# When TensorE and ScalarE read their run-time values: moving register loads and one wait in a sorted mixture-of-experts kernel

## The chip, the cores and the metric

The kernel runs on one core of a Trainium2 chip. The metric is the device time of one execution in microseconds (us). The engines are named as the profile names them: PE is TensorE's matmul side and PEld its weight loads, DVE is VectorE, ACT is ScalarE, POOL is GpSimd, SP is SyncE. A "q" behind an engine (PEldq, ACTq) marks an instruction of that engine's sequencer, which hands instructions to the engine and does the register work itself.

## The reference, cut to what matters

A state-space layer, two layer norms and a mixture of experts over 4096 rows of 256 numbers:

```python
def _L0_attn_ref(x, A, B, C, D, gamma, beta):
    state = jnp.tanh(state @ A.T + xb_t)          # scan over the sequence, xb = x @ B.T
    y = states @ C.T + D * x + x
    return layernorm(y) * gamma + beta
def _L0_ffn_ref(x, ...):
    scores = sigmoid(x @ router_weight.T)         # 8 experts in 2 groups of 4
    # the better group of 4 is chosen, of it the best two experts; comb = their weights
    g, u = x @ w_gate[e], x @ w_up[e]
    routed = sum_e comb[:, e] * ((silu(g) * u) @ w_down[e])
    shared = (silu(x @ sw_gate) * (x @ sw_up)) @ sw_down
    return routed + shared
x = layernorm(x + _L0_attn_ref(x, ...))
x = layernorm(x + _L0_ffn_ref(x, ...))
```

## The kernel before

The 4096 rows are 32 tiles of 128, in 8 batches g of four tiles. After the scan (up to about 75 us of the span) each batch is projected, normalised (`rows`, `scale_rows`, `sum_rows`, `sum_moments`, `normalise`), transposed (`turn_x2`), scored (`logits`, `scores`), routed (`choose_group`, `choose_two`, `weigh`), and **sorted by group**: rows that choose group 0 are copied to the front of `x2_sorted`, the others to its back. A permutation matrix made by `sort_tiles` is multiplied in (`permute`), and ScalarE copies each tile twice, to two places that only the data decide: `offsets` reads those places from `zeros_i` into registers with `value_load`, and `put` copies with `main.placed` as its count. The routing weights go the same way: `turn_comb` multiplies them, `put_comb` copies them into `comb_sorted`, with the count `main.comb_placed`.

The experts' work runs over the sorted rows in ten **passes** i of 2, 2, 4, 4, 4, 4, 4, 4, 2 and 2 tiles. Passes 0 to 8 use one group each and have five **units** j (the shared expert at j = 0, then four routed ones); pass 9 has nine. Which columns and which group a pass takes is decided by the data: GpSimd's `plan(i)` writes them to `pass_i` (count `pass_known`), and TensorE's `take(i)` reads them into registers with two `value_load`s. A unit is `up` (12 matmuls of gate and up projection), ScalarE's silu (L747), VectorE's products (`inner`, L1122 for the shared expert, L1125 and L1129 for routed ones, the latter counting `h_done`), ScalarE's copy to 16 bit (`high`, L756), GpSimd's rest (`low`, L1338) and `down`. The 54 units n = 5i + j are software pipelined: at step n TensorE does `up_main(n + 1)`, `front_early(n)`, `down_main(n - 1)`, `front_late(n)`.

The routing of batch g is spread over the pass before it by `due(n, ahead)`, in an order that each engine's program writes out by hand. In a pass: `scores`, `choose_group` at j = 0; `sort_tiles`, `offsets`, first two `permute`s at j = 1 (the latter on TensorE); the first two `put`s, the other two `permute`s and `choose_two` at j = 2; the other two `put`s, `weigh`, `turn_comb` and `plan` at j = 3, and ScalarE's `normalise` of the batch after; `put_comb`, `turn_x2` and its copies at j = 4. In `turn_x2` the transposes for k = 0 wait for `comb_placed`, as they reuse the bank of the weights (except after the last batch, when there is no `turn_x2`). At the head of a pass `ids` needs the sorted weights, and so do the `spread`s of the units behind it; the products of `up` for j = 0 need only the sorted rows. GpSimd's own long operations at this place are `rows_in` (L1283 and L1288, ahead of passes 2, 3 and 4 only), `low` (L1338) and `low_rows` (L1333). VectorE's `score` (L1023) and `choice` (L1024) are the first steps of `choose_group`.

Of the kernel before, what the change touches and what calls it, by code (L numbers as in the profile page):

```python
# [20 lines left out]
def ssm_moe_kernel(nc, x, A, B, C, D, gamma, beta, router_weight, correction_bias,  # L21
# [8 lines left out]
    T4 = 4  # L30
# [11 lines left out]
    with ExitStack() as ctx:  # L42
# [168 lines left out]
        main, again = Sems("", 3), Sems("again_", 1)  # L211
# [28 lines left out]
        EP = 1 + EPG  # L240
        TILES = [T4 // 2] * 2 + [T4] * (G - 2) + [T4 // 2] * 2
        EXPERTS = [EP] * (G + 1) + [E1]
        KNOWN = list(range(G)) + [G - 1] * 2
        NPASS = len(TILES)
        NP = NPASS - 1
# [3 lines left out]
        UNITS = [(i, j) for i in range(NPASS) for j in range(EXPERTS[i])]  # L249
# [16 lines left out]
        def due(n, ahead, first=0):  # L266

            g, odd = divmod(n + ahead, EP)
            return g if odd == 0 and first <= g < G else None
# [51 lines left out]
        def _(pe):  # L321
# [91 lines left out]
            def permute_main(g, t):  # L413
                if t == 0:
                    pe.wait_ge(perm_ready, g + 1)
                    pe.wait_ge(main.x2_low, g + 1)
                    if g:
                        pe.wait_ge(main.y1_done, 2 * min(g + 2, G))
                if t >= 2 and g:

                    pe.wait_ge(main.placed, g * 2 * T4 + 2 * (t - 1))
                permute(t, perm[:, t, :], ps_rows(g, t), main)
# [14 lines left out]
            def up(n, m, e, group, col, w, sems):  # L437

                if not isinstance(n, int) or n >= 1:
                    pe.wait_ge(sems.silu_done, n)  # L440
                for which, (ps, done) in enumerate(((ps_g, sems.up_g), (ps_u[m % 2], sems.up_u))):
                    if which and (not isinstance(n, int) or n >= 2):
                        pe.wait_ge(sems.gu_done, before(n, m, 1))
                    first = True
                    for k in range(KT):
                        for px, pw in PART:
                            start = e * KT * I + k * I
                            part = bass.ds(group * (EPG * KT * I) + start, I) if group is not None else slice(start, start + I)
                            last = pe.matmul(ps[:, 0:w], up_rows[which][pw][:, part],  # L449
                                             x2_sorted[:, k * 2 + px, bass.ds(col, w)],  # L450
                                             start=first, stop=(k == KT - 1 and (px, pw) == PART[-1]))
                            first = False
                    last.then_inc(done, 1)
# [78 lines left out]
            def take(i):  # L532

                pe.wait_ge(pass_known, i + 1)
                col = pe.value_load(pass_i[0:1, i, 0:1], min_val=0, max_val=N - TILES[i] * P)
                group = pe.value_load(pass_i[0:1, i, 1:2], min_val=0, max_val=1) if i < NP else None
                pe.wait_ge(main.comb_placed, (KNOWN[i] + 1) * 2 * T4)
                return col, group

            taken_at = {}  # L540

            def up_main(n):
                i, j = UNITS[n]
                if j == 0:
                    taken_at[i] = take(i)
                col, group = taken_at[i]
                w = TILES[i] * P
                up(n, n, j, group if j else None, col, w, main)
                if j == 1:
                    pe.wait_ge(main.ids_ready, i + 1)  # L550
                if j:
                    spread(routed(i, j), j, group, col, w, main)
                else:
                    pe.wait_ge(main.h_done, routed(i, 1))
                    ids(col, TILES[i], main)
# [10 lines left out]
            def front_early(n):  # L566

                g = due(n, EP + 1, 2)
                if g is not None:
                    logits(g, main)  # L570
                g = due(n, EP, 1)
                if g is not None:
                    places(g)
                g = due(n, EP - 1, 1)
                if g is not None:
                    for t in (0, 1):
                        permute_main(g, t)
                g = due(n, EP - 2, 1)
                if g is not None:
                    for t in (2, 3):  # L580
                        permute_main(g, t)
                g = due(n, EP - 3, 1)
                if g is not None:
                    turn_comb(g)
# [12 lines left out]

            pe.wait_ge(weights_ready, 3)
            pe.wait_ge(back_made, 1)
            up_main(0)  # L600
            for n in range(NALL):
                if n + 1 < NALL:
# [13 lines left out]
            with pe.If(all_met == 0):  # L616
# [20 lines left out]
                with pe.Fori(0, G // 2) as two:  # L637
                    for half in range(2):
                        g = two * 2 + half
# [18 lines left out]
                        for e in range(E1):  # L658
                            n, m = g * E1 + e, half * E1 + e
# [15 lines left out]
        def _(act):  # L675
# [36 lines left out]
                nc.scalar.activation(th[:, :, :], ps_misc[0][:, 0:T4 * E].rearrange("p (t e) -> p t e", t=T4),  # L712
                                     ACT.Tanh, scale=0.5 / XS).then_inc(sems.th_done, 1)

            def offsets(g):
                act.wait_ge(offsets_known, g + 1)
                return [act.value_load(zeros_i[0:1, g * T4 + t:g * T4 + t + 1], min_val=0, max_val=(g * T4 + t) * P)  # L717
                        for t in range(T4)]

            def behind_copies(done, copy):  # L720

# [76 lines left out]
            normalise(1, 1, main)  # L798
            scores(0, main)
            keep_turned(1, main)  # L800
            at = offsets(0)
            for t in range(T4):
                put(0, t, at)
            scores(1, main)
# [2 lines left out]
            for n, (i, j) in enumerate(UNITS):  # L807
                w = TILES[i] * P
                silu(n, n, w, main)
                if n:  # L810
                    before_i, before_j = UNITS[n - 1]
                    high(n - 1, n - 1, routed(before_i, before_j) if before_j else None, TILES[before_i] * P, main)
                g = due(n, EP, 1)
                if g is not None:
                    high_rows(g, g % 3, main)
                    if g > 1:
                        scores(g, main)
                if j == 0 and i >= 2:
                    finish(i - 2, i % 2, TILES[i - 2], main)
                if j == 1 and i:  # L820
                    sums((i - 1) % 2, TILES[i - 1], (i - 3) % 3, sent_by(i - 3), unit(i, 0), main)
                g = due(n, EP - 1, 1)
                if g is not None:
                    at = offsets(g)
                g = due(n, EP - 2, 1)
                if g is not None:
                    put(g, 0, at)
                    put(g, 1, at)
                g = due(n, EP - 3, 1)
                if g is not None:  # L830
                    put(g, 2, at)
                    put(g, 3, at)
                g = due(n, EP + 2, 2)
                if g is not None:
                    normalise(g, g % 3, main)
                g = due(n, 1, 1)
                if g is not None:
                    put_comb(g, at)
                g = due(n, EP + 1, 2)
                if g is not None:  # L840
                    keep_turned(g, main)
                if (i, j) == (NP, EP):
                    finish(NP - 1, (NP - 1) % 2, TILES[NP - 1], main)
            i, j = UNITS[-1]
# [393 lines left out]
        def _(pool):  # L1238
# [157 lines left out]
            for n, (i, j) in enumerate(UNITS):  # L1396
                if n:
                    low(n - 1, n - 1, TILES[UNITS[n - 1][0]] * P, main)
                g = due(n, EP, 1)
                if g is not None:  # L1400
                    low_rows(g, g % 3, main)
                    note_tiles(g, main)
                g = due(n, 2 * EP - 1, 3)
                if g is not None:
                    deviations1(g, g % 3, main)
                g = due(n, 2 * EP - 2, 3)
                if g is not None:
                    deviations2(g, g % 3, main)
                g = due(n, EP - 3, 1)
                if g is not None:  # L1410
                    plan(g)
                g = due(n, 1, 1)
                if g is not None:
                    watch(g)
                if j == 4 and i:
                    deviations3(i - 1, (i - 1) % 2, TB[i - 1], TILES[i - 1], main)
                if 1 <= i <= G - 5 and j == 4:
                    rows_in(i + 4)
                if j in (0, 1) and i >= 2:
                    half = TILES[i - 2] // 2  # L1420
                    send(i - 2, i % 2, (i - 2) % 3, TB[i - 2], TILES[i - 2], main, range(j * half, (j + 1) * half))
                if (i, j) == (NP, EP):
                    send(NP - 1, (NP - 1) % 2, (NP - 1) % 3, TB[NP - 1], TILES[NP - 1], main)
                if (i, j) == (G - 1, 1):
                    plan(G)
                    plan_last()
# [54 lines left out]
```

## Time and profile before

| | |
|---|---|
| median of 3 runs | 355.1 us (353.13 to 357.61) |
| the profiled execution | 353.79 us, span 352.0 us, so 1.8 us lie outside the span |
| PE busy | 302.4 us, 86% of the span |
| DVE, ACT, POOL busy | 221.0, 185.6, 207.3 us |
| mean granted clock of TensorE | 0.942 of full |
| passes 0 to 9 | from 88.96 us to the end |

No engine is busy all the time; over the passes the work goes round between them, so the question at each place is which wait ends last. Times in the rows are us from the start of the span.

### The profile page before, as it was taken

To read this page: it belongs to the slowest core of one execution; us is meant where nothing else is said; L and a number is where in the kernel's file an instruction comes from. 1 tells how busy PE (TensorE), PEld (TensorE's weight loads), DVE (VectorE), ACT (ScalarE), POOL (GpSimd) and SP (SyncE) were. 2 spreads that over 40 slices of the span, in tenths; PEclk is the share of its full clock that TensorE was granted. 3 is DMA by queue.
4 is the path that set the end of the run, shared out by engine and by line. 5 is a ranking of instruction groups with operands and counts; after the bars stand their busy time and mean duration, and the time that the engine had idled before them with its cause. 6 is when DMAs were issued, how large, how long until landed. Compare 5 with 4: busy or idle time off the path is not lost.

```text
span 352.0 us, 7374 instructions
## 1 busy us (share of the span) xinstructions
PE 302.4 (86%) x2255; PEld 227.5 (65%) x2255; DVE 221.0 (63%) x671; ACT 185.6 (53%) x442; POOL 207.3 (59%) x326
## 2 busy tenths in 40 slices
PE   5999999946696777998998899899899799998940
PEld 4998888846475664764765656476566556787830
DVE  2235998965563893797599499679835723453520
ACT  2565322645357176358349637756864853545420
POOL 8898012453323448648937984678864655578632
PEclk9999999985689986999999999999999999999995
DMA  6992000000000000000000000000001000011001
GB/s 188 343 339 99 0 3 0 2 0 0 0 4 0 2 2 0 19 15 2 0 33 2 2 30 32 2 32 32 0 17 47 3 32 30 7 57 60 32 4 34
DMA packets 6810, 13.19 MB, mean 37 GB/s; under 512 B 1000, under 2 KB 3568, under 8 KB 6768
## 3 DMA queue, kind: packets, MB, share of 16 engines
q1 hardware_dynamic: 5232, 8.47, 7.5%
q0 software_dynamic: 1536, 4.20, 3.4%
q8 instruction: 22, 0.36, 0.4%
q14 instruction: 20, 0.16, 0.2%
HBM read 8.47 MB, written 4.19 MB: 36 GB/s over the span
## 4 chain that ended last, share of the span: by engine, by line
PE 46%; DVE 23%; issue 8%; ACT 7%; POOL 5%; SPq 5%; DMA 2%; ACTq 2%; POOLq 0%; DVEq 0%
PE bank L449 18%; PE bank L472 8%; PE bank L356 5%; PE bank L362 4%; DVE st L964 3%; SPq L290 3%; PE bank L392 3%; PE bank L374 2%; DVE wg L1125 2%; DMA xres<-in_L_attn_x_dram 2%; DVE wu L1129 2%; PE bank L385 2%; POOL out_dram L1382 2%; ACT comb_sorted L740 2%; ACTq L717 2%
## 5 line engine op out<-in xcount | busy, mean ns | idle before, releaser
L1338 POOL TENSOR_TENSOR h<-wu,h 128x512 f16<-128x512 f32 (+1 forms) x54 | 51.0, 947 | 64.0 <-ACT h L756 63.7
L449 PE MATMUL bank<-xT,wg 128*128 x324 | 66.9, 346 | 10.9 <-issue 5.0
L747 ACT ACTIVATE wg<-bank,g_un 128x512 f32<-128x512 f32 (+1 forms) x54 | 32.1, 594 | 79.5 <-PE bank L449 51.9
L472 PE MATMUL bank<-wd,h 128*128 (+1 forms) x504 | 64.7, 275 | 2.1 <-POOL h L1338 2.1
L449 PE MATMUL bank<-xT,wu 128*128 x324 | 65.4, 340 | 0.0
L472 PEld LDWEIGHTS bank<-wd,h 128*128 128x128 f16 x504 | 47.5, 99 | 9.8 <-POOL h L1338 2.6
L449 PEld LDWEIGHTS bank<-xT,wg 128*128 (+1 forms) x324 | 31.3, 101 | 31.8 <-issue 14.7
L1125 DVE SCALAR_TENSOR_TENSOR wg<-bank,u_un,wg 128x512 f32<-128x512 f32 (+1 forms) x44 | 27.3, 620 | 36.1 <-PE bank L449 15.6
L449 PEld LDWEIGHTS bank<-xT,wu 128*128 (+1 forms) x324 | 32.8, 101 | 24.4 <-issue 1.3
L356 PE MATMUL bank<-xT,BT 128*128 128x128 f32 x256 | 39.8, 278 | 0.0
L731 ACT ACTIVATE xT<-bank 128x512 f32 (+1 forms) x64 | 33.6, 613 | 7.9 <-PE bank L409 7.1
L356 PEld LDWEIGHTS bank<-xT,BT 128*128 128x128 f32 x256 | 34.2, 194 | 0.1
L756 ACT ACTIVATE h<-wu 128x512 f16<-128x512 f32 (+1 forms) x54 | 28.7, 532 | 0.9 <-DVE wu L1129 0.9
L1129 DVE TENSOR_TENSOR wu<-bank,wg 128x512 f32<-128x512 f32 (+1 forms) x44 | 25.1, 570 | 1.5
L1136 DVE CAST row_id<-bank 128x4 int32<-128x4 f32 (+1 forms) x10 | 1.6, 161 | 38.4 <-PE bank L464 38.4
L1333 POOL TENSOR_TENSOR wd<-xskip,wd 128x1024 f16<-128x1024 f32 x8 | 17.0, 2130 | 13.1 <-ACT wd L696 13.1
L964 DVE BATCH_NORM_STATS2 st<-xskip 128x6 f32<-128x256 f32 x64 | 22.4, 413 | 0.4
L1382 POOL DMA_INDIRECT out_dram<-z_odd,row_id x16 | 18.4, 1149 | 5.7 <-issue 3.2
L1283 POOL TENSOR_TENSOR xskip<-xres,D_bc 128x1024 f32<-128x1024 f32 x8 | 18.8, 2353 | 1.6 <-PE bank L345 1.6
L1382 POOL DMA_INDIRECT out_dram<-wd,row_id x16 | 16.7, 1046 | 5.1 <-issue 3.2
L683 ACT ACTIVATE states<-bank 128x128 f32<-128x128 f32 x32 | 8.9, 278 | 20.4 <-PE bank L362 20.1
L1288 POOL TENSOR_TENSOR xres<-xres,beta_bc 128x1024 f32<-128x1024 f32 x8 | 18.8, 2356 | 1.1
(186 smaller groups left out, 553.8 us busy)
## 6 DMA issues: line engine op xcount, KB each, us to landing
xres<-in_L_attn_x_dram SPq DMA_DIRECT2D x7, 512.0 KB, 6.1
wd<-in_L_ffn_w_down_dram SPq DMA_DIRECT2D x1, 1024.0 KB, 7.1
xres<-in_L_attn_x_dram SPq DMA_DIRECT2D x2, 256.0 KB, 3.0
out_dram<-wd,row_id POOLq DMA_INDIRECT x16, 2.5
out_dram<-z_odd,row_id POOLq DMA_INDIRECT x16, 2.5
states<-in_L_attn_B_dram SPq DMA_DIRECT2D x1, 128.0 KB, 2.5
D_bc<-in_L_attn_D_dram SPq DMA_DIRECT2D x1, 128.0 KB, 5.0
beta_bc<-in_L_attn_beta_dram SPq DMA_DIRECT2D x1, 128.0 KB, 6.4
```

The costliest lines, as they stand in the source:

```text
L356: pe.matmul(ps_scan[s % 2][:, 0:P], BT[:, k, :], xT[:, k, tile, :], start=(k == 0), stop=False)
L449: last = pe.matmul(ps[:, 0:w], up_rows[which][pw][:, part], x2_sorted[:, k * 2 + px, bass.ds(col, w)], start=first, stop=(k == KT - 1 and ...
L472: last = pe.matmul(ps_y[t // 2][:, (t % 2) * DM:(t % 2 + 1) * DM], h16[:, m % 3, ph, t * P:(t + 1) * P], down_rows[pw][:, rows], start=(fi ...
L731: nc.scalar.activation(x2_sorted[:, :, bass.ds(where, P)], ps_rows(g, t)[:, :].rearrange("p (a c) -> p a c", a=2 * KT), ACT.Copy).then_inc ...
L747: nc.scalar.activation(sg[:, m % 2, 0:w], ps_g[:, 0:w], ACT.Silu, scale=g_un[:, 0:1]).then_inc(sems.silu_done, 1)
L756: nc.scalar.activation(h16[:, m % 3, 0, 0:w], h[:, m % 2, 0:w], ACT.Copy).then_inc(sems.h_high, 1)
L964: nc.vector.bn_stats(st[:, st_k, t, :], src(t)).then_inc(st_sem, 1)
L1125: nc.vector.scalar_tensor_tensor(gu[:, m % 2, 0:w], ps_u[m % 2][:, 0:w], u_un[:, 1:2], sg[:, m % 2, 0:w], ALU.mult, ALU.mult).then_inc(sem ...
L1129: nc.vector.tensor_tensor(h[:, m % 2, 0:w], ps_comb[:, 0:w], gu[:, m % 2, 0:w], ALU.mult).then_inc(sems.h_done, 1)
L1283: nc.gpsimd.tensor_tensor(xskip[:, n * T4:(n + 1) * T4, :], xres[:, n * T4:(n + 1) * T4, :], D_bc[:, :].unsqueeze(1).to_broadcast([P, T4, ...
L1338: nc.gpsimd.tensor_tensor(h16[:, m % 3, 1, 0:w], h[:, m % 2, 0:w], h16[:, m % 3, 0, 0:w], ALU.subtract).then_inc(sems.h_low, 1)
L1382: nc.gpsimd.indirect_dma_start(out_rows, bass.IndirectOffsetOnAxis(row_id[:, ring, t:t + 1], 0), z2s[par][:, t, :], None, bounds_check=N - ...
```

## The change

Four moves, no arithmetic changed. (1) `take(i + 1)`, TensorE's two register loads for the next pass, is issued at j = 3 of pass i ahead of `turn_comb` and `down`, not at the head of the next pass; `take(0)` stands before the first `up`. (2) The wait for `comb_placed` moves from `take` behind the `up` of the pass' unit 0; that `up` waits for `placed` in its place. (3) ScalarE's `offsets`, four register loads at j = 1, become two at j = 2 and two at j = 3, each pair right ahead of the two `put`s that use it. (4) GpSimd's `plan(g)` moves one unit up, from j = 3 to j = 2, and ahead of `deviations2`.

```diff
@@ take(i)
                 group = pe.value_load(pass_i[0:1, i, 1:2], min_val=0, max_val=1) if i < NP else None
-                pe.wait_ge(main.comb_placed, (KNOWN[i] + 1) * 2 * T4)
                 return col, group
@@ up_main(n)
                 if j == 0:
-                    taken_at[i] = take(i)
+                    pe.wait_ge(main.placed, (KNOWN[i] + 1) * 2 * T4)
                 col, group = taken_at[i]
                 w = TILES[i] * P
                 up(n, n, j, group if j else None, col, w, main)
+                if j == 0:
+                    pe.wait_ge(main.comb_placed, (KNOWN[i] + 1) * 2 * T4)
@@ front_early(n)
                     for t in (2, 3):
                         permute_main(g, t)
+                i, j = UNITS[n]
+                if j == EP - 2 and i < NP:
+                    taken_at[i + 1] = take(i + 1)
                 g = due(n, EP - 3, 1)
                 if g is not None:
                     turn_comb(g)
@@ TensorE, before the loop over the units
+            taken_at[0] = take(0)
             up_main(0)
@@ ScalarE
-            def offsets(g):
+            def offsets(g, tiles):
                 act.wait_ge(offsets_known, g + 1)
                 return [act.value_load(zeros_i[0:1, g * T4 + t:g * T4 + t + 1], min_val=0, max_val=(g * T4 + t) * P)
-                        for t in range(T4)]
+                        for t in tiles]
@@ ScalarE, loop over the units
-                g = due(n, EP - 1, 1)
-                if g is not None:
-                    at = offsets(g)
                 g = due(n, EP - 2, 1)
                 if g is not None:
+                    at = offsets(g, (0, 1))
                     put(g, 0, at)
                     put(g, 1, at)
                 g = due(n, EP - 3, 1)
                 if g is not None:
+                    at += offsets(g, (2, 3))
                     put(g, 2, at)
                     put(g, 3, at)
@@ GpSimd, loop over the units
+                g = due(n, EP - 2, 1)
+                if g is not None:
+                    plan(g)
                 g = due(n, 2 * EP - 2, 3)
                 if g is not None:
                     deviations2(g, g % 3, main)
-                g = due(n, EP - 3, 1)
-                if g is not None:
-                    plan(g)
```

## Rows read from the trace of the kernel before

**Rows 1.** The list of waits: who waited for whom, total us, times, longest
```profile
ACT wg L747 <- issue: 27.6, 7, 6.5
PE bank L449 <- issue: 5.0, 6, 1.0
PE bank L430 <- DVE comb L1086: 4.8, 5, 1.5
PE bank L449 <- ACT comb_sorted L740: 4.4, 2, 2.6
```

**Rows 2.** Timeline of PE: first products of passes 0, 1, 2, 3 and 7; brackets: idle before
```profile
88.96 1.46 PE L449 MATMUL bank<-xT,wg 128*128 x6 [2.56 <-ACT comb_sorted L740]
...
111.37 0.83 PE L449 MATMUL bank<-xT,wg 128*128 x6 [0.86 <-issue]
...
137.08 2.74 PE L449 MATMUL bank<-xT,wg 128*128 x6 [0.48 <-issue]
...
166.81 1.47 PE L449 MATMUL bank<-xT,wg 128*128 x6 [1.00 <-issue]
...
281.59 1.47 PE L449 MATMUL bank<-xT,wg 128*128 x6 [1.86 <-ACT comb_sorted L740]
```

**Rows 3.** Register loads of take for pass 4, by line, window 194 to 196.6
```profile
L535 PEldq TENSOR_LOAD <-pass_i x1: 308/308/308, 194.9 to 194.9; - x1
L536 PEldq SEQ_ASSERT  x1: 18/18/18, 196.2 to 196.2; - x1
```

**Rows 4.** Timeline, pass 0: last copies of rows; silu behind the loads
```profile
83.68 3.53 ACT L731 ACTIVATE xT<-bank 128x512 f16<-128x512 f32 x7
...
100.34 0.47 ACT L747 ACTIVATE wg<-bank,g_un 128x256 f32<-128x256 f32 x1 [6.49 <-issue]
```

**Rows 5.** Timeline, pass 4, j = 2 and 3 on PE, DVE and POOL
```profile
214.42 0.75 DVE L1125 SCALAR_TENSOR_TENSOR wg<-bank,u_un,wg 128x512 f32<-128x512 f32 x1
...
214.53 1.47 PE L449 MATMUL bank<-xT,wg 128*128 x6 [0.51 <-ACT wg L747]
...
214.99 1.15 POOL L1338 TENSOR_TENSOR h<-wu,h 128x512 f16<-128x512 f32 x1 [2.54 <-ACT h L756]
...
217.70 0.20 POOL L1313 TENSOR_TENSOR rstd<-mv,eps 128x4 f32<-128x4 f32 x1 [1.56 <-DVE mv L968]
...
220.25 0.69 DVE L1129 TENSOR_TENSOR wu<-bank,wg 128x512 f32<-128x512 f32 x1
...
220.91 0.18 POOL L1362 TENSOR_TENSOR pass_f<-zeros_f,taken 1x1 f32<-1x1 f32 x1
...
222.48 0.29 POOL L1370 TENSOR_SCALAR pass_i<-pass_f 1x1 int32<-1x1 f32 x1
...
222.87 0.40 PE L430 MATMUL bank<-perm,comb 128*128 128x128 f16 x4 [0.81 <-DVE comb L1086]
```

**Rows 6.** Timeline, passes 3 and 4: th, score and choice beside POOL's long operations
```profile
168.59 2.35 POOL L1288 TENSOR_TENSOR xres<-xres,beta_bc 128x1024 f32<-128x1024 f32 x1
170.90 1.16 POOL L1338 TENSOR_TENSOR h<-wu,h 128x512 f16<-128x512 f32 x1
...
171.71 0.38 DVE L1023 TENSOR_SCALAR score<-th 128x32 f32<-128x32 f32 x1 [1.16 <-ACT th L712]
172.02 2.13 POOL L1333 TENSOR_TENSOR wd<-xskip,wd 128x1024 f16<-128x1024 f32 x1
172.13 2.06 DVE L1024 TENSOR_TENSOR choice<-score,cbias_bc 128x32 f32<-128x32 f32 x1
...
198.62 2.36 POOL L1288 TENSOR_TENSOR xres<-xres,beta_bc 128x1024 f32<-128x1024 f32 x1
...
201.43 0.70 DVE L1023 TENSOR_SCALAR score<-th 128x32 f32<-128x32 f32 x1 [1.15 <-ACT th L712]
```

**Rows 7.** Windows over passes 1 and 7 to 8: busy (x count), granted clock
```profile
111.40:137.00 25.60, 20.13 (x159) 16.25 (x159) 19.68 (x71) 14.07 (x35) 12.85 (x28) 0.87 0.01 1
...
281.60:315.30 33.70, 33.69 (x260) 23.79 (x261) 13.84 (x39) 16.38 (x32) 20.52 (x30) 1.00 0.09 33
```
Its columns: length, busy us of PE, PEld, DVE, ACT and POOL, the granted clock of TensorE (1.00 is 2.4 GHz, 0.50 is 1.2 GHz), DMA share and GB/s.

More of the change, by code:

```diff
@@ L800, in _ @@
             keep_turned(1, main)
-            at = offsets(0)
+            at = offsets(0, range(T4))
             for t in range(T4):
```

## The prediction

> **What bounds the kernel now.** I read the list of waits first, then the timeline of PE at the head of each pass, then DVE, ACT and POOL between two heads. The list [rows 1] names what this change is about. PE waits 5.0 us in six places for "issue", which is its own sequencer; 4.4 us in two places for the copied weights; 4.8 us in five places for the weights not yet computed; and ACT waits 27.6 us in seven places for its own sequencer. The timeline [rows 2] shows where: passes 1 to 6 begin with an idle PE of 0.86, 0.48, 1.00, 1.0, 0.85 and 0.85 us behind the last transpose (the three of passes 4 to 6 are not shown, they repeat the row of pass 3 and make up the 5.0), passes 0 and 7 with 2.56 and 1.86 us behind the copies. Those 4.4 us are the only ones at which the wait for `comb_placed` ends last by itself: in passes 2 to 6, and in pass 1, the k = 0 transposes have waited for the same count already, and the change leaves that wait in place.
>
> Between the heads no engine is alone the bound. Over pass 4 the timeline goes PE's products, scores, then VectorE without a gap of note until the weights are done, then PE again. VectorE's L1125 at 214.42 has no bracket, it came straight behind VectorE's own work, while PE's products at 214.53 waited 0.51 us for a silu and `turn_comb` at 222.87 waited 0.81 us for VectorE [rows 5]. So through passes 1 to 4 the loop is head, scores, VectorE's chain, head. In passes 5 to 8 PE has hardly a gap but the heads and is itself the bound; over passes 7 and 8 it is busy for 33.69 of 33.70 us [rows 7].
>
> **Part 1, TensorE's loads (take).** One take runs from 194.9 to 196.2 us, 1.35 us of sequencer time, and the engine stood for 1.0 of it [rows 3], as the sequencer was held until the last wait and could not run ahead. Moved ahead of `turn_comb`, the loads lie behind the `spread` that waits for `h_done`. That product (L1129) ends at 220.94, and `turn_comb` can't start before VectorE's routing weights released it at 222.87 [rows 5]: 1.9 us of cover for 1.35 us of loads, in VectorE's own order, hence the same in every pass that has a `turn_comb`. Cost nothing there; were the cover gone, at most 1.35 us a pass. In passes 7 and 8 there is no `turn_comb`; their two later takes cost between 0 and 1.35 us each, and I take 0, since the lists show no idle PE at the heads of passes 8 and 9 with the loads there today. What the head gives back is the issue wait: 0.86 + 0.48 + 1.00 + 1.0 + 0.85 + 0.85 = 5.0 us, with nothing late behind it, as the `up` of unit 0 needs only sorted rows and registers.
>
> **Part 2, the wait for sorted weights.** Pass 7: its 1.86 us go whole; the copies end before `ids` is due 2.6 us later. Pass 0: `up` now waits for `placed`. Those copies end at 83.68 + 3.53 = 87.21 [rows 4], the products can start at 87.35 instead of 88.96: 1.6 us, not 2.56. Behind the waiting `ids` nothing is held that was not held before. 1.6 + 1.86 = 3.5 us.
>
> **Part 3, ScalarE's loads.** In every pass 0 to 6 the silu of unit 2 stands behind four loads that can't begin before VectorE has written `zeros_i`. With the new order the silu goes ahead. What that is worth is not the 27.6 us: in pass 4 PE gets 0.51 us at 214.53, VectorE nothing, because its L1125 was not waiting [rows 5]. PE's gain then only meets the wait at `turn_comb`, unless VectorE is early too. In pass 0 VectorE itself waits 2.7 us for the silu that starts at 100.34 [rows 4], and ScalarE then runs without a gap to the copied weights. Bounds there are 0.2 us (PE's gap) and 2.7 us (VectorE's); I take 0.7, since the two last `put`s must still follow the `permute`s behind unit 3's products. The first two `put`s begin after two loads instead of after four and two 0.5 us activations, so no `put` becomes later.
>
> **Part 4, plan.** Its seven small operations run from 220.91 to 222.77, 1.9 us [rows 5]. One unit earlier they stand ahead of `deviations2` (L1313), which starts 0.1 us behind its input at 217.70. Today's `low` (L1338) ends at 216.14; plan behind it would end at 218.0 and be 0.4 us late for each of five batches. But that `low` waited 2.54 us for ScalarE's copy, which waited behind the four loads; it now comes about 2.5 us earlier and takes plan with it, to about 215.5. Cost 0; if the cover fails, up to 1.9 us in each of passes 1 to 5. Then `normalise`, the k = 1 transposes, and the silu and the weights' copies queued behind `normalise` on ScalarE are late.
>
> **Part 5, what an earlier head meets on POOL.** In pass 3 `score` (0.38 us) ends 0.03 us after POOL's L1338, and `choice`, issued at 172.13 during L1333 (172.02 to 174.15), takes 2.06 us and ends 0.04 us after it. In pass 4 `score` takes 0.70 and `choice` again 2.06, in a row that repeats pass 3's [rows 6]. Both are small operations that take 0.2 us where nothing of POOL's is running. POOL's L1288, L1338 and L1333 follow each other without a gap, and they start from VectorE's statistics of the pass before, not from PE's head. So a head that comes 1.0 us earlier moves `score` against them. In pass 3: issued at 171.71 - 1.0, that is 0.23 us before L1288 ends at 170.94, done with it; `choice` is then issued during L1338 and done when that ends, at 172.1 instead of 174.19. VectorE wins 2.1 us and is off the path; PE is now next, and what it wins is its 1.0 at the head and the 0.9 us it waited at `turn_comb`. In pass 4 the two gaps are 0.51 and 0.81 us, `score` has only 0.45 us to win to reach L1288's end at 200.98. The Trainium skill (SBUF — State Buffer, "SBUF: two separate sides") says that VectorE and GpSimd share a port pair under an exclusive lock, held for a whole instruction, by which whoever starts first blocks the other. By that rule, the trace agrees that `choice` blocks to L1333's end; it does not say who is next when both wait, and the two readings are my first case and the first rival.
>
> **The sum**, as what each place is early by. Head of pass 1: 1.6 + 0.7 + 0.86 = 3.2. Pass 2's head: 3.2 + 0.48 = 3.7, of which 3.4 pass POOL's row of operations on to VectorE. Head 3: 3.4 + 1.0 = 4.4. Pass 3's `turn_comb`: 4.4 + 0.9 = 5.3. Head 4: 6.3. Pass 4's `turn_comb`: 6.3 + 0.51 + 0.81 = 7.6. Head 5: 7.6 + 0.85 = 8.45. Head 6: 0.85 and a gap of 0.2 at the k = 0 transposes, 9.5. Head 7: 9.5 + 1.86 = 11.3. From there PE runs without a gap [rows 7] and the rest follows it. The profiled execution took 353.79 us, so 353.79 - 11.3 = 342.5; it lies 0.4% below the median of 355.1, and in the median's terms this is **343.8 us**, 3.2% faster.
>
> **Rivals.** (a) *POOL and VectorE make a loop of their own.* If `choice` loses the port to L1333, the 2.1 us aren't won; POOL starts from VectorE and VectorE from POOL's end, and the heads of passes 3 and 4 don't count. Then 3.4 + 0.85 (head 5) + 1.05 (head 6) + 1.86 = 7.1: 346.7, or 348.0 in the median's terms, 2.0% faster. For it: the margin of pass 3 is 0.23 us. Against it: `score`, when waiting at the end of L1338, twice came in ahead of L1333's end. (b) *It is met in one of the two passes*: 9.3 us, 345.8. (c) *TensorE's clock.* The windows show 0.87 granted over pass 1 and 1.00 over passes 7 and 8 [rows 7], and the first six products of pass 2 take 2.74 us against 1.47 in pass 3 [rows 2], the two levels of 1.2 and 2.4 GHz; with the other six it is some 2 us. If the shorter gaps keep the clock at 2.4 GHz there, that and what `choice` wins by it are about 2.5 us more in all: 341. The Trainium skill (TensorE: Matmul & The Clock Gate, Part 1) has the clock follow how busy the array was lately, which would speak for this; the row shows PE busy for only 20.13 of the 25.60 us of pass 1 [rows 7] ahead of the slow products, and the longest wait for VectorE's weights, 1.5 us [rows 1], is among the gaps; VectorE, which makes them, isn't helped. (d) *Slower: plan late.* If POOL reaches `low` no earlier than today, plan pushes `deviations2` by up to 1.9 us in five passes, 9.3 us. With only part 2's and the heads' gain of passes 5 to 7 left that is 353.79 - 7.1 + 9.3 = 356.0, or 357.3, 0.6% slower. It decides from the point where `low` of unit 1 ends less than 1.9 us before the second moments (217.6 in pass 4). The 2.54 us that this `low` waits for ScalarE speak against it. (e) *It does little*: PE's early heads are eaten by other waits (the output's sends on POOL, `low` in the last passes) and 3 to 5 us are left, 350 to 352.
>
> **How the numbers follow.** Chances: forecast 0.40, (a) 0.25, (b) 0.15, (c) 0.08, (d) 0.04, (e) 0.08. Two per cent is about what a measurement of this kernel can tell from no change (its three runs spread by 1.3%). The forecast, (b) and (c) are all beyond 2%, 0.63, and (a) sits on the boundary at 348.0 and gives 0.09 of its 0.25 to faster: 0.72. (a)'s rest, (e) and half of (d) are within, 0.26; slower by over 2% needs (d) with a second cause, 0.02. The range takes in (c) below at 340.5 and (a) with half of its own uncertainty above, 350.
>
> **What would show it.** In the list of waits "PE L449 <- issue" all but gone, and "PE L449 <- ACT comb_sorted" gone; L535's loads just after unit 4's products and before L430, with L430 still released by VectorE. "ACT wg L747 <- issue" gone. `choice` of passes 3 and 4 short, or ended by L1338: forecast; ended by L1333, heads 3 and 4 giving nothing: (a). L1313 starting right behind plan's L1370 and L689 idle for POOL: (d). The first products of pass 2 in 2.6 us: (c). The prediction is wrong if PE waits at L430 grow by what the heads lose, or if the ten heads are early as forecast and the last pass is not.

## The result and the profile after

The changed kernel is faster by one per cent: 350.56 us (median of 4 runs, 349.03 to 351.96) against 355.38 us, ratio 0.9899 with a 95% interval of 0.9855 to 0.9943. In a second set of runs it was 0.9867 [0.9824, 0.9911]. The forecast of 343.8 us and its range of 340.5 to 350.0 both missed it, on the optimistic side; the time lies in the band of rival (e), 350 to 352, which had a chance of 0.08. The profiled execution has a span of 350.1 us against 352.0.

The list of waits of the changed kernel, with the rows that answer to [rows 1]:

```profile
ACT wg L752 <- PE bank L449: 49.0, 32, 3.8
...
PE bank L430 <- DVE comb L1090: 6.9, 6, 1.5
...
PE bank L459 <- DVE wu L1133: 4.7, 8, 1.5
```

The two waits that the change aimed at are gone from TensorE's products: of the 5.0 us of "issue" and the 4.4 us for the copied weights the profile page's group of L449 keeps 1.1 us, for another cause. ScalarE's silu no longer waits for the sequencer; its copies of rows (L736) wait for it for 8.7 us in four places instead. And TensorE's waits for VectorE have grown: `turn_comb` (L430) from 4.8 to 6.9 us, and the `spread` (L459), which waits for VectorE's products of the unit before, from 2.2 to 4.7 us.

```profile
L449 PE MATMUL bank<-xT,wg 128*128 x324 | 65.1, 339 | 1.1 <-ACT xT L736 1.0
```

Where it was lost can be read by laying two points of every pass beside each other in the timelines: the `ids` products (L464), just behind the head of pass p, and `turn_comb` (L430) near its end. Each number is the start in the kernel's profile minus the start in that of before, in us, so -2 is two us early. The last row is the changed kernel's second profile, which began 0.5 us late where the first began 1.2 us late (`turn_comb` of batch 0 at 86.3 and 87.0 instead of 85.8):

| | ids 0 | turn 1 | ids 1 | turn 2 | ids 2 | turn 3 | ids 3 | turn 4 | ids 4 | turn 5 | ids 5 | turn 6 | ids 6 | turn 7 | ids 7 |
|---|---|---|---|---|---|---|---|---|---|---|---|---|---|---|---|
| forecast | -1.6 | | -3.2 | | -3.7 | | -4.4 | -5.3 | -6.3 | -7.6 | -8.5 | | -9.5 | | -11.3 |
| changed | -0.4 | -1.7 | -0.8 | -0.8 | -3.1 | -0.2 | -1.4 | +0.8 | -0.4 | +2.1 | +1.0 | +1.4 | +0.3 | +0.3 | -1.7 |
| again | -1.1 | -2.4 | -3.1 | -2.6 | -4.6 | -2.0 | -3.2 | -1.0 | -2.1 | +0.3 | -0.7 | -0.3 | -1.4 | -1.4 | -3.5 |

The heads from pass 3 on give what they should: from "turn" to the next "ids" the changed kernel wins 1.2 us in passes 3 and 4, 1.0 and 1.1 in passes 5 and 6, and 2.0 in pass 7. The heads of passes 1 and 2 are mixed with TensorE's clock. In the first profile it was granted 0.79 from 104 to 112 us, where the kernel before had 1.00, and head 1 loses 1.0 us; in the second it had 1.00 there too, and head 1 wins 0.6. At the head of pass 2 it is the kernel before that has the low clock (0.58 from 134 to 142 us), so the 2.3 us won there are not the loads' alone. From 145 to 320 us the granted clock is 1.00 in all these profiles. And in every one of passes 2 to 4 the stretch from "ids" to the next "turn", which is VectorE's, takes it away again, with 2.2 to 2.9 us. VectorE is busy for 229.1 us instead of 221.0, with the same 671 instructions. The timeline says which of them became longer. First pass 3, the changed kernel, with VectorE's and GpSimd's rows in order of time (its line numbers are 4 or 5 higher than those of before: L996 is L992, L1342 is L1338):

```profile
170.31 0.47 DVE L1027 TENSOR_SCALAR score<-th 128x32 f32<-128x32 f32 x1 [1.15 <-ACT th L717]
170.70 1.16 POOL L1342 TENSOR_TENSOR h<-wu,h 128x512 f16<-128x512 f32 x1
170.81 1.09 DVE L1028 TENSOR_TENSOR choice<-score,cbias_bc 128x32 f32<-128x32 f32 x1
...
171.82 2.12 POOL L1337 TENSOR_TENSOR wd<-xskip,wd 128x1024 f16<-128x1024 f32 x1
171.94 2.03 DVE L1031 TENSOR_TENSOR more<-choice 128x16 f32<-128x16 f32 x1
...
180.69 1.28 DVE L1118 CAST zeros_i<-zeros_f 1x4 int32<-1x4 f32 x1
180.78 1.17 POOL L1342 TENSOR_TENSOR h<-wu,h 128x512 f16<-128x512 f32 x1
...
181.90 1.65 DVE L996 SCALAR_TENSOR_TENSOR xskip<-xskip,mv,gamma_bc 128x256 f32<-128x256 f32 x4
182.05 3.13 POOL L1366 TENSOR_TENSOR pass_f<-zeros_f,taken 1x1 f32<-1x1 f32 x1
```

Two things are to be seen, beside [rows 6]. `choice` slipped in as forecast: issued at 170.81 during `low`, it ended with it at 171.90, not with `low_rows`. But the next operation, `more`, then stood for 2.03 us until `low_rows` ended at 173.94; before, it took 0.17. Both together end at 173.97, before at 174.40: the slip was worth 0.4 us, not 2.1. And the copy `zeros_i` of four numbers takes 1.28 us, with `low` (L1342) starting 0.09 us behind it and ending 0.02 us ahead of its end. The kernel before has it so:

```profile
181.01 0.15 DVE L1114 CAST zeros_i<-zeros_f 1x4 int32<-1x4 f32 x1
181.08 1.65 DVE L992 SCALAR_TENSOR_TENSOR xskip<-xskip,mv,gamma_bc 128x256 f32<-128x256 f32 x4
...
184.71 1.15 POOL L1338 TENSOR_TENSOR h<-wu,h 128x512 f16<-128x512 f32 x1 [3.63 <-ACT h L756]
```

There `low` came 3.6 us later, since ScalarE's copy that it needs stood behind the four register loads. In pass 2 it is the same (1.31 instead of 0.15); in pass 4 `low` fell on the third of the four L996, which takes 2.02 us (212.58 to 214.60), so that the group takes 3.21 instead of 1.66. This L996 began 0.54 us before the start that is recorded for `low`, and ended 0.30 us behind its end; why it waited although it came first, the rows don't show. In passes 0 and 1 one of VectorE's operations, `zeros_i` and `perm`, pays 0.5 us each in the same way.

```profile
211.79 3.21 DVE L996 SCALAR_TENSOR_TENSOR xskip<-xskip,mv,gamma_bc 128x256 f32<-128x256 f32 x4
...
213.12 1.18 POOL L1342 TENSOR_TENSOR h<-wu,h 128x512 f16<-128x512 f32 x1
```

So the theory behind the experiments, the *port theory*: part 3 takes ScalarE's loads out of the way of `low`, `low` lands on VectorE's operations, and VectorE, whose chain the head waits for, loses 1.2, 1.1 and 1.5 us in passes 2, 3 and 4. Beside it stands the rival (a) of the prediction, the loop of POOL and VectorE, for the heads of passes 2 to 4. The rivals to both: that VectorE's work bounds these passes whatever one does; and that the moved loads, or the copies that now wait for them, hold something up.

### The profile page after: what moved, and what is told of

Its sections match the earlier page's. It is cut to its first block, busy times and chain, and to the rows that moved or that the text cites. A ratio compares the mean times of both kernels' runs of the same rounds, so it can differ in the third digit from the quotient of the medians.

```text
span 350.1 us, 7384 instructions
## 1 busy us (share of the span) xinstructions
PE 301.0 (86%) x2255; PEld 227.7 (65%) x2255; DVE 229.1 (65%) x671; ACT 188.3 (54%) x442; POOL 216.6 (62%) x326
## 4 chain that ended last, share of the span: by engine, by line
PE 42%; DVE 27%; issue 8%; POOL 8%; SPq 6%; ACT 5%; DMA 2%; ACTq 1%; POOLq 0%; DVEq 0%
PE bank L449 15%; PE bank L472 8%; PE bank L356 5%; PE bank L362 4%; DVE st L968 4%; SPq L290 3%; PE bank L392 3%; DMA xres<-in_L_attn_x_dram 2%; DVE wg L1129 2%; DVE wu L1133 2%; POOL out_dram L1386 2%; DVE xskip L1006 2%; PE bank L374 2%; DVE xskip L996 2%; PE bank L385 2%
## 5 line engine op out<-in xcount | busy, mean ns | idle before, releaser
L1342 POOL TENSOR_TENSOR h<-wu,h 128x512 f16<-128x512 f32 (+1 forms) x54 | 51.2, 950 | 51.8 <-ACT h L761 51.4
L449 PE MATMUL bank<-xT,wg 128*128 x324 | 65.1, 339 | 1.1 <-ACT xT L736 1.0
L449 PE MATMUL bank<-xT,wu 128*128 x324 | 64.6, 337 | 0.0
L449 PEld LDWEIGHTS bank<-xT,wu 128*128 (+1 forms) x324 | 32.3, 100 | 23.5
L736 ACT ACTIVATE xT<-bank 128x512 f32 (+1 forms) x64 | 33.7, 608 | 25.3 <-PE bank L409 15.9
L449 PEld LDWEIGHTS bank<-xT,wg 128*128 (+1 forms) x324 | 31.7, 100 | 19.0 <-issue 1.2
L1337 POOL TENSOR_TENSOR wd<-xskip,wd 128x1024 f16<-128x1024 f32 x8 | 17.0, 2130 | 11.3 <-ACT wd L701 11.3
L968 DVE BATCH_NORM_STATS2 st<-xskip 128x6 f32<-128x256 f32 x64 | 22.4, 413 | 0.4
L688 ACT ACTIVATE run_state<-bank 128x128 f32<-128x128 f32 x31 | 8.6, 277 | 20.9 <-PE bank L362 20.9
L1292 POOL TENSOR_TENSOR xres<-xres,beta_bc 128x1024 f32<-128x1024 f32 x8 | 18.8, 2354 | 1.1
```

The lines of the kernel that those rows point to most:

```text
L449: last = pe.matmul(ps[:, 0:w], up_rows[which][pw][:, part], x2_sorted[:, k * 2 + px, bass.ds(col, w)], start=first, stop=(k == KT - 1 and ...
L736: nc.scalar.activation(x2_sorted[:, :, bass.ds(where, P)], ps_rows(g, t)[:, :].rearrange("p (a c) -> p a c", a=2 * KT), ACT.Copy).then_inc ...
L968: nc.vector.bn_stats(st[:, st_k, t, :], src(t)).then_inc(st_sem, 1)
L1342: nc.gpsimd.tensor_tensor(h16[:, m % 3, 1, 0:w], h[:, m % 2, 0:w], h16[:, m % 3, 0, 0:w], ALU.subtract).then_inc(sems.h_low, 1)
```

## The experiments

All ratios are to the kernel before, in the same set of runs, with 95% intervals. Kernels of different sets can be compared by these ratios alone: the first four rows are one set, the next four a second, the last three a third. The span is that of the profiled execution.

| kernel | ratio | span, us |
|---|---|---|
| TensorE's parts only (1, 2 and 4) | 0.9785 [0.9753, 0.9818] | 344.9 |
| ScalarE's loads only (3) | 1.0094 [1.0053, 1.0134] | 358.2 |
| all, `low` held | 0.9800 [0.9745, 0.9855] | 345.8 |
| all, `low` and `low_rows` held | 0.9678 [0.9630, 0.9726] | 341.8 |
| TensorE's parts, `low_rows` held | 0.9672 [0.9622, 0.9723] | 341.1 |
| the moved wait only (2) | 0.9913 [0.9875, 0.9952] | 347.7 |
| TensorE's loads and plan only (1 and 4) | 0.9899 [0.9852, 0.9947] | 349.2 |
| as the fifth, `rows_in` earlier | 0.9714 [0.9666, 0.9762] | 344.4 |
| the same behind batch 0's weights | 0.9616 [0.9574, 0.9658] | 341.3 |
| all, `zeros_i` copied first | 0.9829 [0.9774, 0.9885] | 346.4 |
| the changed kernel again | 0.9867 [0.9824, 0.9911] | 348.4 |

**1. Part 3 undone.** The changed kernel with

```diff
+                g = due(n, EP - 1, 1)
+                if g is not None:
+                    at = offsets(g, range(T4))
                 g = due(n, EP - 2, 1)
                 if g is not None:
-                    at = offsets(g, (0, 1))
                     put(g, 0, at)
@@
-                    at += offsets(g, (2, 3))
                     put(g, 2, at)
```

> The changed kernel with ScalarE's four loads back at unit 1 (part 3 undone); TensorE's loads, the moved wait and the earlier plan stay. Theory (port): the changed kernel gave its gain back because ScalarE's earlier copy of unit 1 starts GpSimd's `low` 2.5 to 3 us earlier, on top of VectorE's last step of `sort_tiles` or first of `scale_rows`, which then wait for its end (1.16, 1.13 and 1.55 us in passes 2, 3 and 4, 0.4 to 0.5 in passes 0 and 1). Then this kernel has zeros_i's copy at 0.15 us in every pass and is 2 to 4 us faster than the changed one: ratio to before 0.980 to 0.985. Rival (VectorE is the bound whatever the heads do, or the loads behind unit 4 hold something up): undoing part 3 can only lose what it gave in pass 0, ratio 0.990 to 1.000.

Measured 0.9785, a little beyond the 0.980 to 0.985 expected: less of a change, and twice the gain. In its timeline of pass 3 `low` is late again and the copy short:

```profile
177.73 0.15 DVE L1119 CAST zeros_i<-zeros_f 1x4 int32<-1x4 f32 x1
177.80 1.66 DVE L997 SCALAR_TENSOR_TENSOR xskip<-xskip,mv,gamma_bc 128x256 f32<-128x256 f32 x4
...
181.42 1.15 POOL L1343 TENSOR_TENSOR h<-wu,h 128x512 f16<-128x512 f32 x1 [3.64 <-ACT h L761]
```

**2. Part 3 alone**, on the kernel before.

```diff
-                g = due(n, EP - 1, 1)
-                if g is not None:
-                    at = offsets(g)
                 g = due(n, EP - 2, 1)
                 if g is not None:
+                    at = offsets(g, (0, 1))
                     put(g, 0, at)
@@
+                    at += offsets(g, (2, 3))
                     put(g, 2, at)
```

> The kernel before with ScalarE's loads alone moved (part 3 alone). Port theory: VectorE loses some 1.15 us in each of passes 2 and 3 and some 1.5 in pass 4 behind the earlier `low`, and wins up to 1 us in pass 0: slower than before by 1 to 3 us, ratio 1.003 to 1.009. Rival: the loads' move is harmless or wins, ratio 0.993 to 1.000.

Measured 1.0094: slower than before, just above the upper end of what the port theory allows (1.009), and outside the rival's. VectorE's waits are where the theory has them: the copy at 1.30 us in pass 2, one L991 at 1.38 us in pass 3 and one at 2.02 us in pass 4. The profiled execution of this kernel has in addition a stretch of low clock (granted 0.50 from 111 to 118 us, where the kernel before had 1.00), so its 358.2 us are no measure; the ratio is.

**3. `low` held.** All four parts, and GpSimd waits ahead of `low` of unit 1 until VectorE is through `sum_rows`:

```diff
+                g = due(n, 2 * EP - 2, 3)
+                if g is not None:
+                    pool.wait_ge(main.z1_done, (g + 1) * T4)
                 if n:
                     low(n - 1, ...)
```

> The changed kernel, and GpSimd waits for VectorE's `sum_rows` (z1_done) ahead of `low` of unit 1 in passes 1 to 5, so that ScalarE keeps its early silu and copy, but `low` can't run beside zeros_i's copy and `scale_rows`. Port theory: zeros_i's copy back at 0.15 us and L996 at 0.47 us each, 3 to 4 us faster than the changed kernel, ratio 0.978 to 0.983. Rival: an added wait wins nothing, ratio 0.990 or above; and if plan now ends behind the second moments, `deviations2` starts late by under 0.5 us a pass.

Measured 0.9800. An added wait, with ScalarE's early silu kept, does about what undoing part 3 does. The interval just meets that of the changed kernel (0.9855), so the rows carry the rest. Pass 3:

```profile
179.03 0.15 DVE L1118 CAST zeros_i<-zeros_f 1x4 int32<-1x4 f32 x1
179.10 1.66 DVE L996 SCALAR_TENSOR_TENSOR xskip<-xskip,mv,gamma_bc 128x256 f32<-128x256 f32 x4
...
182.43 1.15 POOL L1342 TENSOR_TENSOR h<-wu,h 128x512 f16<-128x512 f32 x1 [3.34 <-DVE xskip L1006]
```

From "turn" 2 to "turn" 5 this kernel gains 1.0 us, where the changed one loses 2.9. That tells the port theory from the rest of part 3: ScalarE's loads have their new place here too, and do no harm; what did it is the time at which `low` runs.

**4. The loop of POOL and VectorE.** As 3, and `low_rows` waits for `choose_group`:

```diff
+                    pool.wait_ge(main.choice_step, g * CHOICE_STEPS + 6)
                     low_rows(g, g % 3, main)
```

> As the run before, and GpSimd's `low_rows` (2.1 us) also waits until VectorE's `choose_group` of the batch is done (choice_step). Port theory: at the heads of passes 0 to 6 `score`, `choice` and `more` no longer end with `low_rows`: 0.6 to 2 us a pass, together 4 to 7 us on top of the run before, ratio 0.960 to 0.970; score and choice take 0.15 to 0.2 us except where `low` or `rows_in` are under way. Rival: VectorE's chain is not what the heads wait for, or the later `low_rows` holds up TensorE's permutes: no better than the run before.

Measured 0.9678, within what was expected; the gain on top of experiment 3 is 1.2 percentage points, 4.3 us, at the low end of the 4 to 7 expected (the medians put it at 2.9). **5. The same without part 3 and without the held `low`:**

> The changed kernel with ScalarE's loads back at unit 1 and GpSimd's `low_rows` held until `choose_group` is done, `low` not held. If the heads of passes 2 to 4 gave nothing in the run with TensorE's loads alone because `choice` and `more` end with `low_rows` (the loop of POOL and VectorE), this kernel lets them through: 5 to 8 us faster than that run, ratio 0.955 to 0.965, `turn_comb` early by 1 us or more with every pass. And it has none of the collisions behind the held `low` (1 us each in passes 4, 5 and 6), so it should beat the run with both holds. If instead VectorE's own work bounds these passes, it gains under 2 us, ratio 0.973 or above.

Measured 0.9672, just above the 0.955 to 0.965 expected: 4 us on top of experiment 1 instead of 5 to 8. It is equal to experiment 4 within the intervals; that it would beat it was not borne out. Its own collisions are fewer, but not none (a `pos` of 1.19 us in pass 4, a `total` of 1.16 in pass 5). Pass 3 of this kernel:

```profile
163.68 0.59 DVE L1028 TENSOR_SCALAR score<-th 128x32 f32<-128x32 f32 x1 [1.15 <-ACT th L717]
164.19 1.16 POOL L1343 TENSOR_TENSOR h<-wu,h 128x512 f16<-128x512 f32 x1
...
164.31 1.09 DVE L1029 TENSOR_TENSOR choice<-score,cbias_bc 128x32 f32<-128x32 f32 x1
165.43 0.17 DVE L1032 TENSOR_TENSOR more<-choice 128x16 f32<-128x16 f32 x1
...
166.53 2.14 POOL L1338 TENSOR_TENSOR wd<-xskip,wd 128x1024 f16<-128x1024 f32 x1 [1.19 <-DVE mask L1044]
```

`more` is at 0.17, and `low_rows` waits 1.19 us instead, which costs nothing: its reader is the `permute` of the next unit, and no `permute` of this profile waits for it. The table by places shows what the hold decides:

| | turn 2 | ids 2 | turn 3 | ids 3 | turn 4 | ids 4 | turn 5 | ids 5 | ids 7 |
|---|---|---|---|---|---|---|---|---|---|
| TensorE's parts only | -2.5 | -5.4 | -3.3 | -4.5 | -3.3 | -4.4 | -3.3 | -4.3 | -7.0 |
| with `low_rows` held | -4.4 | -6.9 | -6.9 | -8.0 | -8.8 | -10.0 | -9.3 | -10.3 | -10.7 |

In the first row heads 3 to 5 gain 1.0 to 1.2 us each (head 2 has TensorE's clock in it), and "turn" 3, 4 and 5 all stand at -3.3: that is the loop of rival (a), POOL starting from VectorE's statistics and VectorE released by POOL. With the hold the gains add up to head 5. Behind it passes 5 and 6 take back 1.2 and 1.0 us; the `total` above is in the first of them, the rest stays open.

**6 and 7. The parts by themselves.** The wait only, on the kernel before (`placed` ahead of the first products, `comb_placed` behind them, `take` where it was):

> The kernel before with part 2 alone: `comb_placed` awaited behind the first products, the loads where they were. My sizes: 1.6 us at the head of pass 0 and 1.86 at that of pass 7, none at the other heads, whose transposes have waited already: 3.5 us, ratio 0.990. Rival: pass 0's part is eaten before pass 2, 1.9 us, ratio 0.995.

Measured 0.9913 (3.1 us). The timeline has 1.7 us at the head of pass 0 (ids 0 at -1.7), which come through to pass 7 as 2.2, and 2.0 us at that of pass 7 (ids 7 at -4.2). The interval takes in the rival's 0.995 as well; it is the places that say that pass 0's part is not eaten. The loads and plan only, as experiment 1 with `comb_placed` awaited ahead of the products again:

> TensorE's loads and plan moved (parts 1 and 4), with the wait for `comb_placed` left ahead of the first products. If the loop of POOL and VectorE holds passes 2 to 4, of the 5.0 us only those of heads 1, 5 and 6 and some 0.3 of head 2 come through: 2.9 to 3.3 us, ratio 0.991. If the loads' 5.0 us came through whole: ratio 0.986. Together with the run of the wait alone this must make the run of both (0.9785).

Measured 0.9899 (3.6 us). "turn" 3, 4 and 5 stand at -1.1, -1.1 and -1.0: the heads of passes 3 and 4 give nothing here either, and heads 5 and 6 bring it to -2.7, with a start 0.4 us late; head 7, which waits for the copies again, gives nothing. The interval takes in both expected ratios; the places decide. 0.9913 x 0.9899 is 0.981, within the interval of experiment 1.

**8 and 9. The other half of the collision.** `score` and `choice` of pass 4 still meet `rows_in` and `low`. As 5 (in the expectation "the first run of this call"), with `rows_in(5)` behind `watch(0)` and `rows_in(i + 5)` in the loop for i = 1 and 2:

> As the first run of this call, with GpSimd's `rows_in` of batch 5 moved into its idle stretch before pass 0 and those of 6 and 7 one pass earlier, so that it runs at the heads of passes 2 and 3 only. If `score` and `choice` of pass 4 wait for `rows_in` and the `low` behind it (0.9 and 1.1 us there in the runs so far), VectorE wins 1.5 to 2 us in pass 4: 1 to 2 us faster than the first run of this call, ratio 0.950 to 0.960. Rival: PE is the bound in pass 4 by then, and it wins under 0.5 us.

Measured 0.9714. It was expected 1 to 2 us below experiment 5 and came out 0.4 points above it, within the intervals: no gain, at the least. Pass 4 did what was said, from "turn" 4 to "turn" 5 this kernel wins 2.3 us where experiment 5 wins 0.5. But the two long operations landed on `weigh` of batch 0:

```profile
85.44 2.35 POOL L1288 TENSOR_TENSOR xskip<-xres,D_bc 128x1024 f32<-128x1024 f32 x1
85.50 2.33 DVE L1086 TENSOR_TENSOR comb<-kept,total 128x32 f32<-128x32 f32 x1
...
87.92 2.34 POOL L1293 TENSOR_TENSOR xres<-xres,beta_bc 128x1024 f32<-128x1024 f32 x1
88.09 2.22 DVE L1091 SCALAR_TENSOR_TENSOR comb<-comb 128x32 f16<-128x32 f32 x1
```

So the next one waits for those weights first (`pool.wait_ge(main.comb16_ready, 1)` ahead of `rows_in(5)`):

> As the run with `rows_in` of batch 5 ahead of pass 0, but GpSimd first waits for the routing weights of batch 0 (comb16_ready). In that run the two long operations took turns with the last steps of `weigh` (2.33 and 2.22 us instead of 0.19 each) and cost some 3 us before pass 0, while `score` and `choice` of pass 4 came down to 0.18 and 0.19 and won 1.7 us there. With the wait, VectorE is idle beside the two operations: the 3 us go and the 1.7 us stay, ratio 0.957 to 0.966, the fastest version. Rival: they now hold up something else ahead of pass 0 or 1, and it equals the run without the move, 0.967.

Measured 0.9616, 342.13 us, the lowest of all kernels here and, against the changed kernel in the same set (0.9867), clearly faster. Whether it beats experiment 5 (0.9672) is not settled: their intervals overlap, and in the profiled executions the two are level ("ids" 7 at -10.6 and -10.7). In pass 4 nothing of GpSimd's is near:

```profile
193.28 0.18 DVE L1028 TENSOR_SCALAR score<-th 128x32 f32<-128x32 f32 x1 [1.15 <-ACT th L717]
193.50 0.19 DVE L1029 TENSOR_TENSOR choice<-score,cbias_bc 128x32 f32<-128x32 f32 x1
193.73 0.17 DVE L1032 TENSOR_TENSOR more<-choice 128x16 f32<-128x16 f32 x1
```

**10. Does the collision follow the operation or the place?** The changed kernel, with `zeros_i` copied ahead of the permutation matrix:

> The changed kernel with VectorE's copy zeros_i put ahead of the permutation matrix, so it no longer meets GpSimd's `low`. If any VectorE operation on SBUF alone behind it waits just the same for the end of `low` (the two share a port), the wait of about 1.1 us moves to the next one, the permutation matrix or L996, in passes 2 to 4, and the time stays that of the changed kernel, 0.985 to 0.995. Rival: the copy itself is at fault (its semaphore, its conversion), and the kernel gains 2 to 3 us, ratio 0.978 to 0.983.

The ratio, 0.9829, lies in the rival's range and just below the own one (0.985 to 0.995); its interval, 0.9774 to 0.9885, takes in both, so it decides nothing. The rows do. Pass 3:

```profile
176.46 0.16 DVE L1116 CAST zeros_i<-zeros_f 1x4 int32<-1x4 f32 x1
...
177.14 2.67 DVE L996 SCALAR_TENSOR_TENSOR xskip<-xskip,mv,gamma_bc 128x256 f32<-128x256 f32 x4
...
177.16 1.17 POOL L1342 TENSOR_TENSOR h<-wu,h 128x512 f16<-128x512 f32 x1
```

The copy is short, and the four L996 behind it take 2.67 us instead of 1.65: the wait moved to the next operation. From "turn" 2 to "turn" 5 this kernel loses 2.6 us, the changed one in the same set 2.9, experiment 1 gains 0.8. **11. The changed kernel again:**

> The changed kernel once more, beside its own variants on one chip: ratio 0.985 to 0.994, zeros_i's copy at 1.1 to 1.3 us in two of the passes 2 to 4 and L996 of the third at 2.0 us. If these waits are an accident of one execution they are not there.

0.9867, the copy at 1.31 and 1.29 us in passes 2 and 3, an L996 at 2.01 in pass 4. The waits are no accident of one execution.

## Why the prediction was wrong

**The reading of the heads was right.** 5.0 us of "issue" and 4.4 us for the copies, of which 3.5 were to be had: TensorE's rows show the first gone and the second won (1.7 and 2.0 us in experiment 6, against 1.6 and 1.86). The cover for `take` held: with L535 at 191.7 us, the loads of pass 4 in the changed kernel were over before `turn_comb` began at 193.48, released by VectorE.

**The step that failed is the cost of part 3.** The sum puts it at nothing and enters a gain of 0.7 us. It was worked out for the engine on which the loads run, and for the `put`s behind them; the one thing that it starts earlier, GpSimd's `low` of unit 1, was entered in part 4 as a cover for plan, and only as a gain. What `low` would run beside at its new time was not asked. The rows of VectorE at that time were there: `sort_tiles` and `scale_rows`, operations on SBUF alone, and [rows 6] had shown what such an operation can pay beside one of GpSimd's long ones. By the runs, part 3 costs 3.3 us alone (1.0094) and 3 to 4 us on top of the others (0.9785 against 0.9867 and 0.9899, from other sets).

**The second is part 5, "VectorE wins 2.1 us and is off the path".** `choice` went as forecast, in both passes; but it is one of a row of operations, and the next of them paid 1.86 us of what it had won. Only one operation gets in at a boundary between two of GpSimd's. [Rows 6] had shown it: there `score` got in behind L1338, and the next operation, `choice`, waited for the whole of L1333. The prediction read `score` as a sign for its own case and did not ask who comes behind `choice`. Rival (a), at 0.25, was the right case, with another mechanism at its end than the lost race that it named; the sign that the prediction had set for its forecast, `choice` ended by L1338, came true and decided nothing. The sign that it had set for being wrong, waits at L430 that grow, came true too. The 7.1 us of rival (a) are also the gain in span of experiment 1 (352.0 - 344.9), a kernel in which part 3's cost is absent. That they agree so closely is luck: they hold 0.7 us for part 3, which experiment 1 leaves out, and the clock at the head of pass 2 differs. Experiment 5 bears the loop out: the hold brings the heads of passes 2 to 4 back.

The sum, then: 11.3 us, less 4.2 for the loop, less the three waits of 1.2, 1.1 and 1.5 us behind `low`, leaves 3.3. The measured ratios say 3.6 and 4.7 us. This is an estimate: it leaves out the 0.5 us each of passes 0 and 1, and where the profiled executions started, 1.2 and 0.5 us late. Rival (e), in whose band the time fell, had named other waits (the output's sends, `low` in the last passes); its number was met by another cause.

**The Trainium skill** (SBUF — State Buffer, "SBUF: two separate sides") says that the pair is held for a whole instruction and that the loser "fully blocks". The trace agrees: `zeros_i` ended 0.02 us behind the end of `low`, `more` 0.03 us behind that of `low_rows`. The same section of the Trainium skill lists operations with two SBUF inputs beside those in a two-port mode. Of what waited here `more`, `choice` and L996 have two such inputs; the copy and `score` (2.15 us in pass 2) have one, and no row shows in which mode they ran. Whoever starts first blocks the other, the prediction went on; by the recorded starts that is not so here, where the copy began 0.09 us and L996 0.54 us ahead of `low`, and both waited. Who is next when both wait, on which the forecast had rested a chance, the rows do show: one operation of VectorE's, then GpSimd's next.

**Plan, the clock and the slower case.** Plan was late for nobody in passes 1 to 4, where L1317 still waited for VectorE's moments, for 1.48 us or more behind plan's end. In pass 5 L1317 started at plan's end (248.17), 1.0 us behind the moments, and ScalarE waited 0.18 us for what comes of it. In pass 3 plan's first operation took 3.13 us beside VectorE's L996 and L1006 and cost nothing either: plan still ended 1.4 us ahead of the moments. TensorE's clock came up earlier at the head of pass 2 (granted 0.89 from 134 to 142 us, before 0.58), as rival (c) had it, and `score` then stood for 2.15 us behind `low_rows`; so it is worth nothing while the loop stands.

## What to carry to other kernels

When an edit lets an engine go earlier, list what it will start, on every engine, and look up in the timeline what runs beside that at the new time; an idle engine's late operation may have been late at the right time. Where VectorE bounds a stage, keep GpSimd's long operations on SBUF out of it by a wait of GpSimd's own: holding `low_rows` behind `choose_group` was one line and worth about as much as the whole change (4 us). And a gain at one place of a loop counts only if nothing else closes the loop without it: compare two marks in every pass, not the end alone.

## What the runs showed of the hardware

- Of a row of VectorE's small operations beside two adjoining long ones of GpSimd's, one gets in at the boundary (it ends 0.04 to 0.05 us behind it) and the next waits for the whole of the second: `choice` 1.09 and `more` 2.03 us, in five profiles the same.
- It goes the other way too, but not by the same pattern. In passes 2 and 3 of the changed kernel GpSimd's first operation of plan, on one number, took 3.12 and 3.13 us beside eight of VectorE's (L996 and L1006), and ended with the last of them; in pass 1 it got in between two of the same eight, and took 0.36 us. Which of the two happens is not settled by these runs.
- The order of the recorded starts does not say who waits: `zeros_i` began 0.09 us and an L996 0.54 us ahead of `low`, and they took 1.28 and 2.02 us instead of 0.15 and 0.47.
- Batch-norm statistics and operations that read PSUM kept their length beside GpSimd's long ones: L968 at 1.41 us for four beside `low` (pass 4), L1126 at 0.75 us beside L1292 (pass 3).
